# Attention with routed experts: the last query tile transposed in its own step, values straight behind the next scores

## What is computed

```python
q = x @ w_q; k, v = split((x @ w_kv_down) @ w_kv_up)          # 16 heads of 64
att = softmax(where(causal, q @ k.T * 64 ** -0.5, -inf)); x = x + (att @ v) @ w_out
top_vals, top_idx = top_k(layernorm(x) @ Wr, 2); rw = softmax(top_vals)
x = x + sum over the 2 experts of rw * ((silu(g) * u) @ Wd) * 12 ** -0.5   # g, u = layernorm(x) @ Wg, Wu
```

## Time and profile before

| | |
|---|---|
| Median of 3 runs | 962.83 us (962.78 to 963.06) |
| The profiled execution: time / span from first to last instruction | 964.63 us / 962.8 us |
| TensorE (PE) busy | 900.0 us, 93% |
| VectorE (DVE) busy | 616.4 us, 64% |
| ScalarE (ACT) busy | 585.4 us, 61% |
| GpSimd (POOL) busy | 545.1 us, 57% |

### The profile page before, as it was taken

One profiled execution on the slowest core, in us unless ns is written; L12 is line 12 of the kernel. 1 busy time (PEld: TensorE's weight loads), 2 busy tenths in 40 slices (PEclk: granted clock), 3 DMA queues, 4 the chain that ended last, 5 costly groups with the idle time before them and its releaser, 6 DMA issues. The chain is left out here.

```text
span 962.8 us, 19642 instructions
## 1 busy us (share of the span) xinstructions
PE 900.0 (93%) x5614; PEld 619.0 (64%) x5615; DVE 616.4 (64%) x2375; ACT 585.4 (61%) x1483; POOL 545.1 (57%) x536
## 2 busy tenths in 40 slices
PE   3899999999999999999999999999852999999996
PEld 1566666666666666666666666666531888888885
DVE  2575677677767767776776677677744445544553
ACT  2677677667767766776676677667631444555453
POOL 2555554566466457646655764664553366656655
PEclk9999999999999999999999999999975999999999
DMA  6945330000000000000000000000001233333332
GB/s 198 332 178 232 139 87 1 7 13 17 1 13 20 4 7 12 18 1 12 21 3 7 12 18 1 12 20 5 3 31 34 31 47 49 46 44 47 44 44 28
DMA packets 43417, 44.32 MB, mean 46 GB/s; under 512 B 4288, under 2 KB 35904, under 8 KB 43216
## 3 DMA queue, kind: packets, MB, share of 16 engines
q0 software_dynamic: 16528, 26.03, 11.2%
q1 hardware_dynamic: 26816, 17.39, 6.5%
HBM read 15.28 MB, written 28.12 MB: 45 GB/s over the span
## 5 line engine op out<-in xcount | busy, mean ns | idle before, releaser
L318 POOL TENSOR_TENSOR prob<-prob,row_inv 128x512 f32<-128x512 f32 (+3 forms) x256 | 321.7, 1257 | 289.0 <-DVE row_inv L615 285.1
L445 ACT ACTIVATE prob<-prob,neg_max 128x256 f32<-128x256 f32 (+3 forms) x512 | 281.0, 551 | 171.3 <-DVE neg_max L608 171.3
L937 PE MATMUL low_ps<-PT,v_sb 128*64 128x512 f32 (+3 forms) x1024 | 153.6, 443 | 2.4 <-ACT PT L451 2.4
L405 POOL DMA_INDIRECT out<-prob,meta_row x71 | 111.0, 1563 | 35.1 <-issue 35.1
L937 PEld LDWEIGHTS low_ps<-PT,v_sb 128*64 128x64 f32 x1024 | 68.4, 137 | 94.8 <-issue 64.9
L926 PEld LDWEIGHTS low_ps<-ident,prob 128*128 128x128 f32 x768 | 86.5, 140 | 60.2 <-issue 50.1
L926 PE MATMUL low_ps<-ident,prob 128*128 128x128 f32 x768 | 108.4, 277 | 3.1 <-DVE neg_max L608 2.4
L821 DVE TENSOR_TENSOR prob<-mid_ps,prob 128x512 f32<-128x512 f32 x71 | 49.1, 692 | 84.1 <-ACT prob L541 52.7
L445 ACT ACTIVATION_READ_ACCUMULATOR prob<-prob,neg_max 128x1 f32 x512 | 96.7, 189 | 0.0
L608 DVE CUSTOM_DVE_ANT_0 prob<-mid_ps,mask 128x128 f32<-128x128 f32 (+1 forms) x256 | 93.5, 421 | 0.4 <-issue 0.2
L608 DVE CUSTOM_DVE_ANT_0 prob<-top_ps,mask 128x512 f32<-128x512 f32 x128 | 83.3, 689 | 12.3 <-PE low_ps L926 12.3
(11 more groups left out here) (168 smaller groups left out, 1699.7 us busy)
## 6 DMA issues: line engine op xcount, KB each, us to landing
routed_rows<-W_dn POOLq DMA_DIRECT2D x8, 2080.0 KB
routed<-routed_rows SPq DMA_DIRECT2D x71, 65.0 KB
X<-in_L_attn_x SPq DMA_DIRECT2D x8, 256.0 KB, 5.5
W_ffn<-in_L_ffn_Wg SPq DMA_DIRECT2D x8, 256.0 KB, 5.0
W_ffn<-in_L_ffn_Wu SPq DMA_DIRECT2D x8, 256.0 KB, 5.3
W_dn<-in_L_ffn_Wd SPq DMA_DIRECT2D x8, 256.0 KB, 4.5
out<-X SPq DMA_DIRECT2D x8, 256.0 KB, 2.3
out<-prob,meta_row POOLq DMA_INDIRECT x71
```

The costliest lines, as they stand in the source:

```text
L318: nc.gpsimd.tensor_tensor(p_pair(i), p_pair(i), row_inv[:, i, :].unsqueeze(2).to_broadcast([P, 2, P * (i + 1)]), ALU.mult).then_inc(S["nor ...
L405: nc.gpsimd.indirect_dma_start(out=out, out_offset=bass.IndirectOffsetOnAxis(ap=meta_row[:, q:q + 1], axis=0), in_=eo_sb[q], in_offset=Non ...
L445: nc.scalar.activation(p_at(i, h), p_at(i, h), ACT.Exp, bias=neg_max[:, i, h:h + 1], scale=-1.0, accum_out=row_sum[:, i, h:h + 1]).then_in ...
L937: last = nc.tensor.matmul(y_ps[h * HD:(h + 1) * HD, j * P:T], v_sb[:, half, j, o + h * HD:o + (h + 1) * HD], PT[:, h, j, j:NT, :].rearrang ...
```

## The change

- **TensorE.** The values of step n - 1 stand directly behind the scores of step n; then project, T1, output projection, T2, T0, the value chunk, and T3 of step n at the end. Before, T3 of step n - 1 stood behind the scores, then project, values, chunk, T1, output projection, T0, T2. The first step transposes tile 3 too.
- **PSUM.** T2 moves to low_ps (both banks), T3 to top_ps. So T2 waits for t1_copied, scores 3 for t3_copied, scores 1 for t2_copied, and the values for the maxima of tile 1 (y_ps shares a bank with its scores). Several waits on TensorE go, as others imply them.
- **ScalarE.** The exps of tile 3 come before qk_copy, v_copy later, and t3_copy of the same step is the last of the step.
- **VectorE.** inv 2 and y_copy come before the blocks of `pre_` and `post_`; behind these inv 3 and the copies of T1, T2, T0.
- **POOL.** The four norms of a step are together, and the scatters behind norm 3 at k = 7, 8 (three each) and 1 (two).

```diff
-        SCATTER_EARLY, SCATTER_LATE = {7: 0, 8: 2, 1: 4}, {7: 1, 8: 3, 1: 5, 2: 6, 3: 7}
+        SCATTERS = {7: (0, 3), 8: (3, 6), 1: (6, 8)}
...
-            ps, o = {2: (top_ps, 0), 3: (low_ps, 0)}[i]
-            return ps[:, :].rearrange("p (h n) -> p h n", h=2)[:, :, o:o + w].rearrange("p h (j q) -> p h j q", q=P)
+            ps = {2: low_ps, 3: top_ps}[i]
+            return ps[:, :].rearrange("p (h n) -> p h n", h=2)[:, :, 0:w].rearrange("p h (j q) -> p h j q", q=P)
...
# POOL's step
-                if n:
-                    norm(n - 1, 3)
...
-                norm(n, 1)
+                for i in ORDER:
+                    norm(n, i)
                 if fills and k < FILLS:
                     fill(k)
-                norm(n, 0)
-                if post is not None and k in SCATTER_LATE:
-                    scatter_at(post, k, SCATTER_LATE[k])
-                norm(n, 2)
+                if post is not None and k in SCATTERS:
+                    scatter_at(post, k)
...
# ScalarE's step
+                if cur:
+                    exps(n, 1)
+                    exps(n, 0)
                 if post is not None and k == 1:
                     post_out(post)
                 if cur:
-                    exps(n, 1)
-                    exps(n, 0)
-                if prev:
-                    t3_copy(n - 1)
-                if cur:
                     exps(n, 2)
+                    exps(n, 3)
                 if nxt:
                     qk_copy(n + 1)
-                if cur:
-                    exps(n, 3)
-                if v:
-                    v_copy(n + 3, (k + 3) % NP // NT, (k + 3) % NT)
...
+                if v:
+                    v_copy(n + 3, (k + 3) % NP // NT, (k + 3) % NT)
...
+                if cur:
+                    t3_copy(n)
...
# VectorE's step
                     inv(n, 1)
                     maxes(n, 3)
                     inv(n, 0)
+                    inv(n, 2)
+                if prev:
+                    y_copy(n - 1)
                 if pre is not None:
...
                 if cur:
-                    inv(n, 2)
-                if prev:
-                    y_copy(n - 1)
-                if cur:
+                    inv(n, 3)
                     t_copy(n, 1)
-                    inv(n, 3)
+                    t_copy(n, 2)
                     t_copy(n, 0)
-                    t_copy(n, 2)
...
# TensorE: waits of scores, transposes and values
                 if i == 1:
-                    seen(pe, S["qk_copied"], n + 1)
-                    seen(pe, S["t1_copied"], n)
-                    seen(pe, S["y_copied"], n - 1)
+                    seen(pe, S["qk_copied"], 1 if n == 0 else 0)
+                    seen(pe, S["t2_copied"], n)
...
                 if i == 3:
-                    seen(pe, S["t2_copied"], n)
+                    seen(pe, S["t3_copied"], n)
...
-                if i == 3 and cur:
-                    seen(pe, S["max_done"], 8 * (n + 1) + 2)
-                if i == 3 and not cur:
+                if i == 2:
                     seen(pe, S["t1_copied"], n + 1)
-                    seen(pe, S["y_copied"], n)
-                if i == 1:
-                    seen(pe, S["t3_copied"], n)
...
-                seen(pe, S["t3_copied"], n + 1)
-                for i in range(NT - 1):
+                if cur:
+                    seen(pe, S["max_done"], 8 * (n + 1) + 2)
+                for i in range(NT if not cur else 0):
                     seen(pe, S[f"t{i}_copied"], n + 1)
...
# TensorE's step
                     for i in ORDER:
                         scores(n, i)
-                if prev:
-                    transposes(n - 1, 3, cur)
+                values(n - 1, (k - 1) % NP, cur)
...
                 if nxt:
                     project(n + 1, (k + 1) % NP, m + (k + 1) // NP)
-                if prev:
-                    values(n - 1, (k - 1) % NP)
-                if v:
-                    seen(pe, S["qk_copied"], n + 2)
-                    v_chunk(n + 3, m + (k + 3) // NP, (k + 3) % NP // NT, (k + 3) % NT)
                 if cur:
                     transposes(n, 1)
...
+                project_out(n - 1, (k - 1) % NP)
                 if cur:
+                    transposes(n, 2)
                     transposes(n, 0)
-                    transposes(n, 2)
+                if v:
+                    v_chunk(n + 3, m + (k + 3) // NP, (k + 3) % NP // NT, (k + 3) % NT)
+                if cur:
+                    transposes(n, 3)
```

More of the change, by code:

```diff
@@ L336, in post_scatter, with scatter_at @@
                         in_=routed[:, k, t, :], in_offset=None).then_inc(S["rows_written"], 16)
-            def scatter_at(post, k, part):
+            def scatter_at(post, k):
                 b = post if k > 6 else post - 1
                 if b >= 0:
-                    post_scatter(b, part, part + 1)
+                    post_scatter(b, *SCATTERS[k])
             def fill_last():
@@ L365, in step @@
                     post_rstd(post)
-                if post is not None and k in SCATTER_EARLY:
-                    scatter_at(post, k, SCATTER_EARLY[k])
-                norm(n, 1)
+                for i in ORDER:
+                    norm(n, i)
                 if fills and k < FILLS:
                     fill(k)
-                norm(n, 0)
-                if post is not None and k in SCATTER_LATE:
-                    scatter_at(post, k, SCATTER_LATE[k])
-                norm(n, 2)
+                if post is not None and k in SCATTERS:
+                    scatter_at(post, k)
             pre_rstd(0)
@@ L386, in _ @@
                 step(NP * (B - 1) + k, k, post=B - 2)
-            norm(STEPS - 1, 3)
-            post_scatter(B - 2, 2, 8)
+            post_scatter(B - 2, 3, 8)
             post_rstd(B - 1)
@@ L456, in v_copy, with step @@
                 nc.scalar.activation(v_sb[:, half, t, :], mid_ps[:, bank * T:(bank + 1) * T], ACT.Copy).then_inc(S["v_copied"], 1)
-            def step(n, k, cur=True, prev=True, nxt=True, pre=None, post=None, v=True):
+            def step(n, k, cur=True, nxt=True, pre=None, post=None, v=True):
+                if cur:
+                    exps(n, 1)
+                    exps(n, 0)
                 if post is not None and k == 1:
@@ L514, in _ @@
             exps(0, 3)
+            t3_copy(0)
             for k in range(1, NP + 1):
@@ L876, in project @@
             def project(n, pair, b):
-                seen(pe, S["xTlo_done"], b + 1)
+                if n == 0:
+                    pe.wait_ge(S["xTlo_done"], 1)
                 seen(pe, S["max_done"], 8 * (n - 1) + 6)
@@ L885, in v_chunk @@
             def v_chunk(n, b, half, t, bank=0):
-                seen(pe, S["xTlo_done"], b + 1)
+                if half == 0 and t == 0:
+                    seen(pe, S["xTlo_done"], b + 1)
                 passes(mid_ps[:, bank * T:(bank + 1) * T], [XT[:, a, b * T + t * P:b * T + (t + 1) * P] for a in range(2)],
@@ L906, in scores, with transposes @@
                 last.then_inc(S["s_ready"], 1)
-            def transposes(n, i, cur=True):
+            def transposes(n, i):
                 seen(pe, S["norm_done"], NT * n + POS[i] + 1)
-                if i == 3 and cur:
-                    seen(pe, S["max_done"], 8 * (n + 1) + 2)
-                if i == 3 and not cur:
+                if i == 2:
                     seen(pe, S["t1_copied"], n + 1)
-                    seen(pe, S["y_copied"], n)
-                if i == 1:
-                    seen(pe, S["t3_copied"], n)
                 if i == 0:
@@ L927, in transposes, with values @@
                 last.then_inc(S[f"t{i}_ready"], 1)
-            def values(n, pair):
-                seen(pe, S["t3_copied"], n + 1)
-                for i in range(NT - 1):
+            def values(n, pair, cur):
+                if cur:
+                    seen(pe, S["max_done"], 8 * (n + 1) + 2)
+                for i in range(NT if not cur else 0):
                     seen(pe, S[f"t{i}_copied"], n + 1)
@@ L945, in project_out, with step @@
                                  skip_group_check=True).then_inc(S["out_ready"], 1)
-            def step(m, k, cur=True, prev=True, nxt=True, pre=None, post=None, v=True):
+            def step(m, k, cur=True, nxt=True, pre=None, post=None, v=True):
                 n = NP * m + k
@@ L1032, in _ @@
                 v_chunk(t, 0, 0, t, t % 2)
-            for i in (1, 0, 2):
+            for i in (1, 2, 0, 3):
                 transposes(0, i)
```

4 lines of the change are left out of this document (removed).

## The result

| | before | after |
|---|---|---|
| Median | 962.84 us (962.78 to 963.06) | 994.45 us (993.05 to 995.38), 4 runs |
| Span of the profiled execution | 962.8 us | 993.0 us |
| Start of the span to S2 | 45.99 | 50.17 (+4.2) |
| Rest of image 0 | 62.07 | 62.45 (+0.4) |
| Images 1 to 6 | 507.3 | 528.1 (+20.8) |

The ratio is 1.0326, 95% interval [1.031, 1.0343]: slower by 31.6 us, where I had forecast 12.7. S is again the start of a step's first score matmul, and S0, S1, ...

The account below looks back on a forecast made before the run. TensorE's queue was taken to bound the kernel, at 10.28 us a step. Images +7.0, image 0 -0.5, start +3.0 and last image +3.2 gave +12.7 on 962.8: 975.5 us, range 966 to 983.

Parts of the forecast that it names:

- Its likeliest case: The forecast itself, 975.5 us, 1.3% slower, given a chance of 0.68.
- TensorE's own order, -0.29: TensorE's step: three seams between kinds of tile instead of four, 9.99 us, 0.29 less.
- T2 behind T1's copy, 0.2: T2 in low_ps waits for T1's copy: starts at 7.64, due at 7.45, net -0.08 in a plain step.
- rivals A and B: Seam from scores to values: A, costs nothing, 966, chance 0.12; B, gives time back, faster than before, chance 0.04.
- The blocks, +1.17 an image: VectorE's image blocks, now behind y_copy, delay T1's copy or results TensorE needs: +1.17 us an image, +7.0 for six.
- Start, +3.0: First step: T3(0) now behind norm 3, next scores later by 3.5, 0.5 given back: +3.0 us.
- Last image, +3.2: Last image: values wait for tile 1's maxima after a weight split, +0.8 in four steps: +3.2 us.
- Image 0, -0.5: Image 0 has only the light blocks: -0.5 us.
- T3, scores 3, scatters: covered: T3's wait for tile 3's norm, scores 3's for t3_copied and the moved scatters were to cost nothing.
- Rival C: Tile 3's chain (maxima, exps, inv 3, norm, T3) does not fit into its step: up to +9, 984; chance 0.12.
- Rival D: Blocks do not delay T2, as VectorE is 1 us ahead of the offsets: about 961; chance 0.04.

Follow-up runs that it names:

- e1: The changed kernel with T0 put ahead of T2 on TensorE; 987.17 us, ratio 1.0262.
- e8: The changed kernel with POOL's norm of tile 2 cut to 32 of 384 columns of each head, queue orders kept; one execution, 973.01 us.
- e9: The kernel before with one part of the change alone, inv 2 ahead of the image blocks; one execution, 988.91 us against 964.49.
- e5: The changed kernel, ScalarE reordered: step 0's tile 3 exps before value copies, last image's weight split right behind copy of q and k; 984.14 us.
- e6: The changed kernel with e1, e5, blocks of k = 1, 3, 4 before inv 2 and y_copy, those of 2, 6 behind T1's copy; 960.53 us.
- e7: e6 with the choose block (k = 5) behind T1's copy and the ranks behind the value chunk; 957.02 us, ratio 0.9933.

## Why the prediction was right or wrong

**Direction right, size wrong**: +31.6 us against +12.7, and 994.45 is above the range (966 to 983). Its likeliest case is what the trace shows, with one mechanism missing that none of the rivals had. Measured for forecast, by stretch of the two spans: six images +20.8 for +7.0, image 0 +0.4 for -0.5, start +4.2 for +3.0, last image +5.6 for +3.2; and S63 to the end, which had no term, -0.8 (-2.0 up to the last output projection, where only the kernel before has a stretch at half clock and the last T3 still to come; +1.2 behind it, where the stretch at half clock is 37.5 long instead of 30.7; how the 2.0 divides is not shown).

- *TensorE's own order, -0.29, and T2 behind T1's copy, 0.2.* The sum is right, 10.20 for 10.2, and T2 starts at 7.63 for 7.64. Its parts are each off by 0.1: e1, where nothing waits in a plain step, puts the bare order at 10.09 instead of 9.99 (T2 was due at 7.53, not 7.45), and the wait at 0.10. No gain comes from the seam between scores and values, so rivals A and B fall.
- *The blocks, +1.17 an image.* **The step that failed**; the runs show +3.47. It took each block's length from rows in which POOL rested or ran a short norm, and the change moves inv 2, and by that norm 2, beside them. The order is in the diff, and inv 2's move stood ahead of y_copy in my own account; I priced VectorE's queue and not what inv 2 sets off. With norm 2 out of the way (e8) the steps are 10.81, 10.44, 11.04, 11.52 and 10.36, forecast 10.9, 10.7, 11.0, 11.5 and 10.7: the queue arithmetic was good to 0.1 at k = 2, 4 and 5 and up to 0.34 too long at k = 3 and 6. So two errors stand against each other: the images gained 20.8 where I had 7.0, and of the 20.8 the holds beside norm 2 are 18.1 and the queue only 2.7. The rows for both were there. In the kernel before, the first picked of k = 6 takes 0.53 and the next 0.18, and of the four xn_sb the second takes 0.64 and the others 0.33. Both end at the end of norm 0 (timeline of before, 346.5 to 346.6):

```profile
346.24 0.61 POOL L318 TENSOR_TENSOR prob<-prob,row_inv 128x256 f32<-128x256 f32 x1 [0.57 <-DVE row_inv L615]
346.36 0.53 DVE L731 TENSOR_TENSOR picked<-chosen,pos 128x32 f32<-128x32 f32 x1
```

So the lengths that I read, 1.39 for k = 3 and 1.86 for k = 6, already held 0.31 and 0.35 of a hold beside norm 0, which the new order no longer has there; this is about what those two steps were put too long.
- *Start, +3.0.* The order costs about what I said: from S0 to S2 the profiled run of after takes 27.23, before 21.80. Of these 5.4, 1.3 is that norm 3 starts 12.88 after S0 (35.82) instead of 11.58 (35.77), and 0.9 that T3 takes 1.87 and not 0.97. Both lie in stretches at the half clock (the granted clock of after is 0.5 from 19.9 to 26.7 and from 36.9 to 40.4; before it is 1.0 there). e1 and e9 bear this out: e1 has the change's order and no early half-clock stretch, and norm 3 starts 11.53 after S0; e9 has the old order and such a stretch (20.3 to 27.1), and it starts 12.96 after. The other 3.2 is the wait for norm 3. (T2 of this step waits 2.5 before it, as T1's copy now stands behind inv 3.) The span gained 4.2, as S0 itself came 1.25 earlier in that run.
- *Last image, +3.2.* Measured +5.6 up to S63. The mechanism is right (values at 4.08 after S, forecast 4.1), the sum was short: it had only the splits, and not the last image's own blocks of k = 2, 4, 5 and 6, with their holds; with norm 2 small (e8) this stretch is 79.0, so 3.0 of the 5.6 hang on that norm. e5 takes out 5.9, and leaves the last image where it was before (76.1 against 76.4).
- *Image 0, -0.5.* Measured +0.4 from S2 on, and its one step with a held block is most of the difference: k = 3 is 11.47 there too, against 10.71 before and a forecast of 10.7.
- *T3, scores 3, scatters: covered.* Right. T3 waits for a norm nowhere in the images.
- *Rival C* came nearest to the result (984), by a wait that the images do not have; that is no merit of it. *Rival D* was refuted by y_copy, which starts at 4.78 as forecast.

The hold, first as the runs show it: in after the first xn_sb ends 0.08 after norm 2, dest, picked and xn2 end 0.03, 0.05 and 0.08 after it, and with norm 2 small all four are short. VectorE's copies out of PSUM, its maxima, bn_stats (0.28 with and without) and X<-post_ps,X (0.68 beside norm 2, 0.67 in the kernel before) are not held. This agrees with the Trainium skill (SBUF — State Buffer, SBUF: two separate sides), which calls the port pair that VectorE and GpSimd share an exclusive lock: whichever starts first keeps it for its whole instruction, and this touches only VectorE's instructions in a two-port mode, or with two SBUF inputs against a GpSimd instruction that reads SBUF. That the lock is what holds these instructions is the page's reading; the rows show that they end with the norm. The page speaks against this change; by it the move of inv 2 was a cost of up to 1.47 us a block, and I had weighed only the rule on TensorE's tiling modes.

The second xn_sb of the kernel before fits as well: the first ran while norm 0 started and took 0.33, the second took 0.64, to 0.09 behind norm 0's end. The other direction, POOL held by VectorE, does not show: norm 0 started 0.17 before that first xn_sb ended and took 0.63, against 0.61 to 0.62 in the other steps. What stays open is the part of a scatter. e9's dest starts 0.29 before the norm that it ends with (the held xn_sb of k = 3 0.75 before), while the scatter still runs, so by that rule something of the scatter must have held it first; yet the last xn_sb of k = 3 in the kernel before (314.15 to 314.49) ran beside a scatter (from 314.07) at 0.33. And no run tells why the early stretches at half clock come in some executions and not in others; e6, e7 and the kernel before have none between S0 and S2.

## What to carry to other kernels

When an edit moves a small instruction ahead, ask what it releases on another engine and what will then run beside it. In this kernel VectorE's tensor_tensor with both inputs in SBUF and its tensor_scalar from SBUF to SBUF, when they started while a norm on GpSimd ran, ended only with it or after it, even at 8 elements and in every one of the eleven traces up to S63; reciprocals, bn_stats and what reads PSUM did not wait. Price the former from a row in which both run, and look for such a row among the outliers of a group (0.53 next to 0.18). Where a queue is held up, put first what TensorE waits for, and put behind it the blocks that nobody needs in that step: with the blocks so placed, and ScalarE's order mended at both ends (e7), the order that lost 3.3% gains 0.7%, though at the start and the end of attention and not in the six images between.
